# Routing weights laid over the experts' rows by transfers through memory, three convolution rooms, and new hand orders, in a fused graph-attention and mixture-of-experts kernel

## What is computed

```python
sg = xf @ shared_gate_w.T;  su = xf @ shared_up_w.T
shared_out = silu(sg) * su @ shared_down_w.T
topk_idx, w, _ = _route(xf, router_w, correction_bias)      # 4 of 16 experts per token
combine = zeros((S, E)).at[arange(S)[:, None], topk_idx].add(w)
g = einsum('sc,ech->esh', xf, gate_w);  u = einsum('sc,ech->esh', xf, up_w)
hw = silu(g) * u * combine.T[:, :, None]
routed = einsum('esh,ehc->sc', hw, down_w)
return shared_out + routed
```

## Time and profile before

| | us |
|---|---|
| median of three executions | 986.1 |
| the profiled execution, device time | 988.29 |
| its span in the trace | 986.5 |
| PE busy in the span | 928.2 (94%) |
| DVE, ACT, POOL busy | 602.0, 413.6, 207.0 |
| PE's share of the chain that ended last | 83% |
| all transfers, share of 16 DMA engines | 5.0% |

### The profile page before, as it was taken

How to read it: one execution, slowest core, us unless ns; L and a number is a source line. 1 busy time by engine, 2 the same in 40 slices (tenths; PEclk the granted TensorE clock), 3 DMA queues, 4 the chain that set the end, 5 groups by cost and what they waited for, 6 DMA issues and landing times.

```text
span 986.5 us, 20130 instructions
## 1 busy us (share of the span) xinstructions
PE 928.2 (94%) x8254; PEld 823.7 (83%) x8254; DVE 602.0 (61%) x1630; ACT 413.6 (42%) x796; POOL 207.0 (21%) x184
## 2 busy tenths in 40 slices
PE   5697879999999999999999999999999999999997
PEld 3486657988978989798988989788898889888997
DVE  4648865756685377744786467852778447764532
ACT  3543513722564226551365415642265523622431
POOL 2004100022401123121312123011231213112222
PEclk9799889999999999999999999999999999999999
DMA  9100000000000100001000010000000000000000
GB/s 324 49 1 22 1 1 1 2 23 13 1 12 1 33 2 11 2 1 33 2 12 2 1 33 1 12 2 30 5 12 1 2 12 1 12 1 12 12 12 11
DMA packets 14378, 17.78 MB, mean 18 GB/s; under 512 B 1073, under 2 KB 12721, under 8 KB 14289
## 3 DMA queue, kind: packets, MB, share of 16 engines
q1 hardware_dynamic: 14288, 16.51, 5.0%
HBM read 12.31 MB, written 4.19 MB: 17 GB/s over the span
## 4 chain that ended last, share of the span: by engine, by line
PE 83%; DVE 7%; ACT 6%; issue 2%; POOL 1%; DMA 1%; SPq 0%; POOLq 0%; DVEq 0%; ACTq 0%
PE ring L1314 8%; PE d_ps L506 5%; PE g_ps L506 5%; PE d_ps L507 4%; PE d_ps L508 4%; PE g_ps L508 4%; PE u_ps L507 4%; PE u_ps L508 4%; PE u_ps L506 4%; PE g_ps L507 4%; PE ring L1182 4%; PE ring L1297 3%; PE num L1211 3%; PE ring L506 3%; PE ring L508 3%; PE ring L507 3%
## 5 line engine op out<-in xcount | busy, mean ns | idle before, releaser
L652 POOL TENSOR_TENSOR hl<-hb,hh 128x512 fp32r<-128x512 f32 x96 | 122.9, 1281 | 492.2 <-ACT hh L796 492.2
L1150 DVE TENSOR_TENSOR hb<-sl,u_ps 128x512 f32<-128x512 f32 x88 | 60.2, 684 | 109.8 <-PE u_ps L508 47.9
L506 PE MATMUL d_ps<-hh,down_h 128*128 128x256 f32 x384 | 113.5, 296 | 1.9 <-POOL hl L652 1.9
L506 PE MATMUL g_ps<-normed_h,gate_h 128*128 128x256 f32 x352 | 109.3, 310 | 0.4 <-DVE hb L1154 0.2
L507 PE MATMUL d_ps<-hl,down_h 128*128 128x256 f32 x384 | 107.5, 280 | 0.0
L508 PE MATMUL d_ps<-hh,down_l 128*128 128x256 f32 x384 | 107.5, 280 | 0.0
L796 ACT ACTIVATE hh<-hb 128x512 fp32r<-128x512 f32 x96 | 60.9, 634 | 108.1 <-DVE hb L1154 88.6
L508 PE MATMUL g_ps<-normed_h,gate_l 128*128 128x256 f32 x352 | 99.2, 282 | 0.0
L507 PE MATMUL u_ps<-normed_l,up_h 128*128 128x256 f32 x352 | 99.1, 282 | 0.0
L508 PE MATMUL u_ps<-normed_h,up_l 128*128 128x256 f32 x352 | 99.1, 282 | 0.0
L506 PE MATMUL u_ps<-normed_h,up_h 128*128 128x256 f32 x352 | 99.1, 281 | 0.0
(11 more groups left out here) (340 smaller groups left out, 2144.5 us busy)
## 6 DMA issues: line engine op xcount, KB each, us to landing
out_x<-kept SPq DMA_DIRECT2D x16, 256.0 KB, 2.1
x_s<-in_x SPq DMA_DIRECT2D x14, 256.0 KB, 3.0
raw_weights<-in_gateT SPq DMA_DIRECT2D x4, 384.0 KB, 8.4
raw_weights<-in_upT SPq DMA_DIRECT2D x4, 384.0 KB, 9.8
raw_weights<-in_down SPq DMA_DIRECT2D x4, 384.0 KB, 12.4
cheb_s<-in_cheb SPq DMA_DIRECT2D x3, 256.0 KB, 4.7
raw_weights<-in_wqkvT SPq DMA_DIRECT2D x2, 384.0 KB, 6.4
shared<-in_x SPq DMA_DIRECT2D x2, 256.0 KB, 2.8
```

Source lines behind the costliest of these rows:

```text
L506: eng.matmul(ps, wh, xh, start=start, stop=False, **how)
L652: pool.tensor_tensor(hl[:, j % 2, :], hb, hh[:, j % 2, :].bitcast(F32), ALU.subtract).then_inc(*ffn_pool.mark(p, f"lo{j}"))
L1150: dve.tensor_tensor(hb, sl, gate_up(p, j)[1][:, :], ALU.mult).then_inc(*ffn_dve.mark(p, f"h{j}"))
```

## The change

1. `spread`, its piece, its memset, the cm matmuls and `whl` go. Step cb transposes the plain weights, ACT copies 16 rows to `comb`, SP writes them to a buffer in memory (`keep_rows`), waits for that, and for each routed step reads them back, each expert's row 64 times (`spread_rows`, two transfers of 64 partitions), into one of two halves of `over`. DVE multiplies hb by `over`. The next gu waits for h and no longer for w.
2. There are three rooms: pair 1 gets one inside raw and in sl and hb, pairs 2 to 7 share the third. So pair 2's x is loaded at the start, and ten of the fourteen pieces are loaded only when pair 1's tail is through.
3. The splits become steps of their own (high, low) in the order, `hot` has 24 steps for 23, and OPENING, BODY and CLOSING are written anew. SP follows the same order as the other engines.

```diff
-CHAINS["warm"] = [f"hot{i}" for i in range(23)]
+CHAINS["warm"] = [f"hot{i}" for i in range(24)]
+CHAINS["high"] = [f"high{i}" for i in range(14)]
+CHAINS["low"] = [f"low{i}" for i in range(14)]
...
 OPENING = """
-    0:gn 1:gn 0:xg 0:hot0 0:hot1 0:hot2 1:xg 0:hot3 0:xT0 0:M 0:xT1 0:Y0 0:hot4 0:prod 0:hot5 1:xT0 0:Epre 1:M 0:hot6
...
-    0:hot8 0:st1 1:sp0 0:xb 1:rv0 0:o0 0:o1 1:sp1 0:tc0 1:st0 0:tc1 1:rv1 0:z1 1:xb 0:z2 1:Y1 0:hot9 0:z3 1:st1 1:o0
-    1:o1 1:tc0 0:tok0 1:tc1 1:z1 0:tok1 0:hot10 2:gn 0:nrm 0:hot11 1:z2 0:xl0 0:xl1 0:hot12 0:hot13 2:xg 0:k0 0:k1
...
+    0:gn 0:xg 1:gn 1:xg 0:xT0 0:M 0:hot0 0:xT1 1:xT0 0:Y0 0:high0 2:gn 0:prod 0:low0 0:Epre 0:high1 1:M 0:hot1 1:xT1
...
+    0:o0 1:sp1 1:st0 0:low1 0:low2 0:o1 0:high3 0:tc0 1:rv1 0:tc1 0:low3 2:Y0 0:z1 0:hot12 0:hot13 0:hot14 2:prod 1:Y1
+    0:z2 1:st1 0:z3 1:o0 2:Epre 0:tok0 0:tok1 0:nrm 1:o1 0:xl0 1:xb 0:hot15 0:xl1 2:Eexp 1:tc0 0:k0 0:k1 0:v1 0:q0
+    2:Erep 0:v0 0:kt 0:q1 0:hot16 1:tc1 0:hot17 2:lr 1:z1 0:dent 2:p2 0:hot18 0:kv 1:z2 0:rd 0:S00 2:sp0 0:V00 1:z3
+    2:rv0 0:S01 0:hot19 2:sp1 0:at0 0:V01 0:high4 0:S10 0:low4 0:hot20 0:V10 0:low5 0:S11 2:st0 0:hot21 0:high5
...
 BODY = """
-    +1 tok0 tok1 lg nrm +1 gn +2 xg xl0 +1 xl1 +1 r1 +2 xT0 M k0 k1 v1 xT1 +1 Y0 r2 q0 r3 v0 kt q1 prod silu +1 r4 +1
-    Epre dent cb kv +1 rd +2 Eexp S00 +2 Erep +1 lr +3 p2 +2 sp0 rv0 sp1 +1 st0 V00 +2 rv1 Y1 +3 S01 +2 st1 +1 at0 +1
...
+    +1 tok0 tok1 lg +1 gn +1 nrm xg +4 r1 +1 xT0 xl0 xl1 M r2 xT1 +2 k0 k1 v1 q0 v0 r3 +2 Y0 silu +1 r4 prod cb Epre
+    Eexp kt q1 +2 Erep dent kv +1 lr +1 rd +3 S00 +1 p2 +3 V00 S01 +2 sp0 rv0 sp1 +1 st0 at0 V01 +1 rv1 Y1 +1 xb +1
...
             for i in range(len(PIECES)):
+                if i == EARLY_PIECES:
+                    sp.wait_ge(tail_dve.of(1), tail_dve.at(1, "n30"))
+                    sp.wait_ge(tail_pool.of(1), tail_pool.at(1, "n31"))
                 sp.dma_start(PIECES[i][3], PIECES[i][0]).then_inc(piece_loaded[i], 16)
...
+            def keep_rows(p):
+                sp.wait_ge(route_act.of(p), route_act.at(p, "cb"))
+                sp.dma_start(rows_kept[p % 2], comb[:, :]).then_inc(rows_written, 16)
+                sp.wait_ge(rows_written, 16 * (p + 1))
+
+            def spread_rows(p, r):
+                j = ROUTED_STEPS[r]
+                if p or r > 1:
+                    user = (p, ROUTED_STEPS[r - 2]) if r > 1 else (p - 1, ROUTED_STEPS[r - 2])
+                    sp.wait_ge(ffn_dve.of(user[0]), ffn_dve.at(user[0], f"w{user[1]}"))
+                first = 2 * chunks_of(j)[0]
+                toks = slice(j // HALF * L, (j // HALF + 1) * L)
+                for e in range(2):
+                    source = rows_kept[p % 2].rearrange("(c e) l -> e c l", e=2)[e, first // 2:first // 2 + 2, toks]
+                    sp.dma_start(over[64 * e:64 * e + 64, r % 2].rearrange("p (c l) -> p c l", c=2),
+                                 source.unsqueeze(0).to_broadcast([64, 2, L])).then_inc(over_loaded[r % 2], 16)
...
                 if kind == "w" and routed(j):
-                    dve.wait_ge(ffn_pe.of(p), ffn_pe.at(p, f"cm{j}"))
+                    r = ROUTED_STEPS.index(j)
+                    dve.wait_ge(over_loaded[r % 2], 32 * (p * len(ROUTED_STEPS) // 2 + r // 2 + 1))
                     dve.wait_ge(ffn_dve.of(p), ffn_dve.at(p, f"h{j}"))
-                    dve.tensor_tensor(hb, hb, gate_up(p, j)[0][:, :], ALU.mult).then_inc(*ffn_dve.mark(p, f"w{j}"))
+                    dve.tensor_tensor(hb, hb, over[:, r % 2, :], ALU.mult).then_inc(*ffn_dve.mark(p, f"w{j}"))
...
-                        pe.wait_ge(ffn_dve.of(p), ffn_dve.at(p, f"w{i}" if routed(i) else f"h{i}"))
+                        pe.wait_ge(ffn_dve.of(p), ffn_dve.at(p, f"h{i}"))
...
-                if kind == "h" and routed(j):
-
-                    pe.wait_ge(route_act.of(p), route_act.at(p, "cb"))
-                    pe.wait_ge(ffn_act.of(p), ffn_act.at(p, f"si{j}"))
-                    for x, chunk in enumerate(pair):
-                        last = pe.matmul(gate_up(p, j)[0][:, x * L:(x + 1) * L], spread[:, chunk, :], comb[:, toks], start=True, stop=True)
-                    last.then_inc(*ffn_pe.mark(p, f"cm{j}"))
```

More of the change, by code:

```diff
@@ L120 @@
[L120 to L124, removed]
@@ L132 @@
-    exp +1
+    +1 tok0 tok1 lg +1 gn +1 nrm xg +4 r1 +1 xT0 xl0 xl1 M r2 xT1 +2 k0 k1 v1 q0 v0 r3 +2 Y0 silu +1 r4 prod cb Epre
+    Eexp kt q1 +2 Erep dent kv +1 lr +1 rd +3 S00 +1 p2 +3 V00 S01 +2 sp0 rv0 sp1 +1 st0 at0 V01 +1 rv1 Y1 +1 xb +1
+    st1 o0 o1 tc0 +1 S10 +1 V10 +1 S11 +2 tc1 V11 z1 at1 +1 z2 wo0 wo1 +3 tk0 tk1 +4 nrm2 z3 +4 xn0 xn1 +2 exp +1
 """
 CLOSING = """
-    +1 7:tok0 7:tok1 6:lg 7:nrm 6:r1 6:r2 +2 7:xl0 +1 7:xl1 6:r3 +2 6:silu 6:r4 +2 7:k0 7:k1 7:v1 +1 7:q0 +1 7:v0 7:kt
@@ L140 @@
+    7:r4 +1 7:cb +29 7:exp +16
 """
@@ L168, in program @@
         put(int(word.split(":")[0]) if ":" in word else None, word.split(":")[-1])
-    once = [(p, n) for p in range(PAIRS) for c in CHAINS if c != "warm" for n in CHAINS[c]]
-    assert sorted(out) == sorted(once + [(0, n) for n in CHAINS["warm"]])
+    every = [(p, n) for p in range(PAIRS) for c in CHAINS if c not in ONCE for n in CHAINS[c]]
+    assert sorted(out) == sorted(every + [(0, n) for c in ONCE for n in CHAINS[c]])
     for c in CHAINS:
-        if c == "warm":
+        if c in ONCE:
             continue
@@ L196, in routed @@
     return chunks_of(j)[0] < ROUTED
+ROUTED_STEPS = [j for j in range(STEPS) if routed(j)]
 GROUPS = [f"{b}{lc}" for b in range(2) for lc in range(2)]
-NO_TILE = ["xg", "Eexp", "rv0", "rv1", "nrm", "nrm2", "at0", "at1", "exp", "silu"] + ["V" + g for g in GROUPS] + CHAINS["tail"] + CHAINS["ffn"] + CHAINS["warm"] + "lg r1 r2 r3 r4 cb".split()
+NO_TILE = ["xg", "Eexp", "rv0", "rv1", "nrm", "nrm2", "at0", "at1", "exp", "silu"] + ["V" + g for g in GROUPS] + CHAINS["tail"] + CHAINS["ffn"] + [n for c in ONCE for n in CHAINS[c]] + "lg r1 r2 r3 r4 cb".split()
 RING = 4
@@ L534, in graph_attention_moe @@
                            raw[:, wide * (10 + k):wide * (11 + k)].rearrange("p (c n) -> p c n", c=3)))
-        ONE_PART = 3 + 4
+        ONE_PART = 3 + 5
         BOTH_PARTS = 3 + 8
-        ROUTED_DOWN = {2: 13, 3: 14, 4: 15, 5: 15}
-        HIGH_AT = {"0:xT1": 2, "0:Epre": 2, "0:p2": 2, "1:Epre": 2, "0:rv1": 1, "0:Y1": 2, "1:Y1": 2, "1:o0": 2}
-        LOW_AT = {"0:Erep": 2, "0:p2": 2, "1:p2": 2, "0:st1": 2, "1:st1": 6}
[L542 to L546, removed]
-            order = [w for w in (f"{q}:{n}" for q, n in PROGRAM) if w in at]
-            before = sum(at[n] for n in order[:order.index(here)])
-            return range(before, before + at[here])
-        PREP_POOL = 12
-        assert len(PIECES) == sum(HIGH_AT.values()) == sum(LOW_AT.values()) + 1
+        ROUTED_DOWN = {2: 13, 3: 14, 4: 14, 5: 14}
+        PREP_POOL = 11
+        assert len(PIECES) == len(CHAINS["high"]) == len(CHAINS["low"])
         block = ctx.enter_context(nc.Block())
```

174 lines of the change are left out of this document (95 added, 79 removed).

## The result

| | before | after |
|---|---|---|
| median of four executions each, side by side | 987.3 us | 959.5 us |
| ratio, 95% interval | | 0.972 (0.9695 to 0.9741) |
| profiled execution, its span | 988.3, 986.5 | 960.8, 959.2 |

The account below looks back on a forecast made before the run. PE's issue bounds the kernel from 165 us on, the first pairs' dependences before. Terms 20.5 + 4 + 4 - 3 + 15 = 40.5 us off 988.3 give 947.8, median forecast 946; range 928 to 967, more than 8 in 10.

Parts of the forecast that it names:

- the rival in which the opening gives nothing: Opening: pair 0's chain stays as long with three convolutions threaded in, or late pieces hold it; 961 us, chance 0.20.
- Step 1: Routed steps: 128 cm matmuls go, 15.4 us of issue plus 5.1 of silu waits; gain 20.5 us, bounds 15.4 and 25.4.
- Step 2: Loop gu, h, gu: gu waits for h and not w, dropping 0.69 us; worth nothing unless the new order uses it.
- Step 3: PE's order: fewer changes between three-part and plain fp32 matmuls, 253 for 337; gain 4 us, bounds 0 and 9.
- Step 4: Middle turns: gn placed before nrm removes PE's 0.87 us wait for DVE; gain 4 us over five turns, bounds 0 and 5.
- Step 5: Weights through memory: covered except at each pair's first routed step; loss 0.4 us a turn, 3 us in all, bounds 0 and 24.
- my rival (3 us a turn): Middle turns: round trip through memory late by 3 us each, lr and dn wait; 967 us, chance 0.09.
- Step 6: Opening to pair 0's first gu: z3 5, splits 2, nrm 7, clock 1; gain 15 us, bounds 25 gain and 5 loss.

Follow-up runs that it names:

- old order, no products, no round trip: Kernel before with weights through memory and no cm matmuls, each pair's first two reads taking the previous pair's rows; 973.0 us.
- memory way in the old order: Kernel before with weights sent through memory, no cm matmuls and gu waiting for h; order, two rooms and pieces kept old; 1008.9 us.
- moved steps back: Kernel after with pair 1's second token half (tok1) and pair 2's output convolution (o1) put back ahead of the first gu; 964.5 us.
- the closing moved: Kernel after with one split (low13) 10 places earlier and the last pair's routing (xn0 to cb) two steps earlier; 960.7 us.
- the opening moved: Kernel after with low13 and the last pair's routing earlier, and pair 1's group sums behind pair 0's first transposes and M; 964.7 us.

## Why the prediction was right in direction and 13 us too large

The result lies in the stated range, and close to the 961 of the rival in which the opening gives nothing. That is no support for the rival: the opening gave 15.9 us. Both the middle and the opening came near their forecasts in part by luck, since errors of single terms cancel. For the middle turns the traces show it. A turn less all waits of PE in it over 0.1 us is what PE has to issue:

| one middle turn, us | length | PE's waits | issue |
|---|---|---|---|
| before | 115.46 | 2.65 | 112.81 |
| before, products twice | 117.10 | 2.65 | 114.45 |
| old order, no products, no round trip | 113.83 | 2.91 | 110.92 |
| after, nrm ahead of gn | 113.25 | 2.50 | 110.75 |
| after | 112.16 | 1.39 | 110.77 |

The other turns of each run but the fifth agree within 0.3 us. Against my terms a turn gave 1.9 us of products' issue for 1.9, some 0.15 of the waits for silu for 0.64, 1.1 at gn for 0.8, 0.15 of changes of kind for 0.5, and nothing lost to the transfers for 0.4: 3.3 for 3.5. The waits in the turn of after are these two:

```profile
PE ring L1213 <- ACT kept L764: 0.8, 1, 0.8
PE ring L1227 <- DVE filters L986: 0.6, 1, 0.6
```

**Step 1, the products: issue right, waits mis-sized.** I counted 20.5 us; taking them away gave 13.3, doubling them cost 14.7. The issue of a turn fell by 1.9 us, as the 8 x 0.24 read from starts say. The 5.1 us of waits for silu, 0.64 a turn, were not a gain: in the old order, with the products gone, PE waited 0.9 us a turn at rd; in the new one PE's waits fell by 1.26 us a turn, of which 1.1 are gn's. My reason, that the next gu needs only h, which is ready earlier, looked one step ahead and not three. The lower bound that I gave, 15.4, was the better value.

**Step 2, gu waits for h: costed at nothing, which only the old order bears out.** In it the release is worth 0.2 us a turn. In the new one it is what lets 8.9 us of other work stand between h and w, and taking it back costs 71 us. I wrote "nothing, unless the new order uses it" and then did not look whether it does. The sum was not hurt, since the order was judged with the release in place, but I had ranked the parts of the change wrongly.

**Step 3, fewer changes of kind: put too high.** From the run in the old order without the products to after, the issue of a turn falls by 0.15 us, where I had 0.5. So most of what the new order gives in a turn is waits of PE (2.91 us to 1.39) and not issue.

**Step 4, the wait of gn: right, and under its worth.** 4 us forecast; 1.1 us a turn and 6.8 in the whole by the run that puts nrm back.

**Step 5, the transfers: the landing right, the place wrong.** The reads land in 3.0 us, and later steps never wait. The way from copy to w took 5.7 to 6.3 us in pairs 1 to 5 for my 6.2: the copy 0.6, the write 1.6 and not 2.1, the reads 3.5 to 4.1 for 3.5. Of the 0.4 us a turn that I charged nothing shows on PE in the middle, but only just: the run with two writes puts the slack at 0.1 us, and the waits that it brings are at lr and dn, the two places that I had named. The loss is in the last pair, 1.0 us of wait and what follows from it, which my sum did not treat apart. The price of my rival (3 us a turn) came true in the old order at twice its size, though no transfer was late there: the order covered less of the way, and I had not counted the clock. The 2.0 us of fixed cost that the prediction takes from the Trainium skill (DMA: Bandwidth & Descriptors, "Anatomy of one DMA") are given there for transfers that GpSimd issues; SP issues these, and its write of 32 KB landed in 1.6 us.

The Trainium skill (SBUF — State Buffer, "SBUF: two separate sides") says that a DVE instruction with two SBUF inputs and a POOL instruction that reads SBUF shut each other out. I had weighed this rule down. One row in each of five turns agrees with it: w lasts 1.63 us for 0.69 when it starts while POOL's product of two SBUF tiles runs.

```profile
582.25 1.28 POOL L675 TENSOR_TENSOR kept<-kept,filters 128x512 f32<-128x512 f32 x1
...
582.45 1.63 DVE L1185 TENSOR_TENSOR hb<-hb,weights_over_hidden 128x512 f32<-128x512 f32 x1
```

POOL ends at 583.53, and 0.69 us later, at 584.22, is where w ends (584.08) within 0.15 us. Five such rows are 4.7 us of DVE and none of PE, so the price in the sum, nothing, was right.

**Step 6, the opening: right in its sum by luck, wrong in what it gives back.** The first gu came 14.1 us earlier and the first h 15.9, for 15. But the three parts of the sum were all off. Up to tok0 (z3 and the splits) I had 7 us and it gave 3.4; from tok0 to k (nrm) I had 7 and it gave 5.6; from k to the first gu I had 1 and it gave 5.1 (65.0 us for 70.1). No run separates what gave the 5.1.

The sentence that failed is "so little of the gain is given back behind it". The second half of pair 2's o (16 matmuls for the filters and its other products) now stands behind the first gu; by starts it is 5.6 us of PE, and tok1 of pair 1 another 0.6. Pair 0's stretch has waits of 2.7 us where it had 0.8. Less 2.6 us of products by starts, that is 5.5 of the 6.2 us by which the stretch grew. Yet moving the work back does not help, for there it covers pair 1's norm; so the steps are rightly placed, and it was my ledger that booked the opening's whole gain as gain.

**The last two pairs.** I gave each of the eight pairs the same 2.7 us. Pair 7 has no other work beside it, so the round trip shows: its issue fell by 1.6 us and its waits grew by 1.2. Pair 6 takes over part of pair 5's routing: by starts the 16 router matmuls are 1.8 us more, about ten matmuls of gu and dn at the edges of the stretch 1.2 more, and PE's waits are 1.6 us for 1.1, against 2.4 us less for the products. Net of the 1.5 us that the five turns gave beyond the forecast, the two pairs are 5.2 us of the missing 13.2.

## What to carry to other kernels

A wait taken off the bound engine is a gain only if no later wait takes its place: count the issue that goes, and the wait only if what releases each of the next steps has been looked at too. When a trace is at hand, part each turn into issue and waits before and after; it prices a change of order that no single run isolates. A dependence that costs nothing today may be the one that a new order stands on; ask of each released wait how far the work can now be moved apart. When a rewritten order shortens the opening, look at what has been moved behind its end before booking the gain, and cost the first and the last pair by themselves.

## What the runs showed of the hardware

The price of an idle stretch of TensorE can be more than its length. In a part that ran at the full clock, idle times of 2.54 us (memory way in the old order), 3.13 (moved steps back), 3.55 (products back in the new order) and 4.50 (gu waits for w) each came with 3.4 or 6.8 us at the 1.2 GHz level, which began between 1.1 us before the end of the wait and 0.8 after it. There half the time is lost: up to 1.7 or 3.4 us on top. The waits of 1.77 and 1.0 us in the kernel after had no such stretch behind them. Near 2 us it went both ways. The 1.97 us before tok0 in after and the 2.17 at cb above had none. In the kernel after, one of 2.06 us in the opening had, and so had one of 2.17 us near the end:

```profile
134.78 0.49 PE L1242 MATMUL num<-shared,v_s 128*32 128x128 f32 x9 [2.06 <-DVE shared L1072]
...
135.45:142.25 6.80, 5.99 (x54) 4.30 (x49) 4.94 (x9) 0.00 (x0) 0.00 (x0) 0.50 0.39 123
```

The same wait of 2.06 us had none within 8 us in the profiles of the closing moved and of the opening moved. One of 1.99 us in the run where gu waits for w had one in four turns of five, while in the run with the products back in the new order the same wait had it in none:

```profile
551.72 0.39 PE L519 MATMUL g_ps<-normed_h,gate_h 128*128 128x256 f32 x1 [1.99 <-DVE hb L1185]
...
553.00:556.50 3.50, 3.50 (x25) 3.26 (x27) 0.30 (x1) 0.60 (x1) 0.69 (x1) 0.51 0.24 80
```

So where a wait's bounds reach 2 us, its upper price has to hold the clock as well: the rival of 3 us a turn was one of 6. The 2.8 us named in the expectation of the run with two writes is not a bound below which nothing happens.
